# Weight scales of a low-rank feed-forward made for two chunks at a time, in products of 256 columns instead of 128

## The chip, the cores and the metric

The kernel runs on one core of a Trainium2 chip. The metric is the device time of one execution, in microseconds (us). The core has TensorE (PE, matmuls; PEld is its weight load), VectorE (DVE), ScalarE (ACT), GpSimd (POOL) and SyncE (SP), which issues nearly all DMAs here. Each engine works through its own list of instructions in order, and waits at semaphores for the others. Matmul results lie in PSUM, eight banks of 128 x 512 float32; only two of them, numbers 6 and 7, are at stake here.

## What is computed

2048 tokens of width 512 go through a small state-space stack of four layers, a feed-forward, an attention of 32 heads, and the same feed-forward again, each on a normalized input and added to x. The change touches the first feed-forward alone. Its weights are products of a raw matrix and a low-rank matrix of scales:

```python
B, S, H, I, R = (4, 32, 512, 1792, 4)

def _anemll_linear(x, w, su, sv):
    w_eff = w * (su @ sv)
    return jnp.einsum('bsh,oh->bso', x, w_eff)
a = _anemll_linear(x, gate_w, gate_su, gate_sv)
b = _anemll_linear(x, up_w, up_su, up_sv)
d = jax.nn.silu(a) * b
return _anemll_linear(d, down_w, down_su, down_sv)
...
x = x + _L0_attn_a_ref(_layernorm(x, axis=-1), ...)
x = x + _L0_ffn_ref(_layernorm(x, axis=-1), ...)
x = x + _L0_attn_b_ref(_layernorm(x, axis=-1), ...)
x = x + _L0_ffn_ref(_layernorm(x, axis=-1), ...)
```

## The kernel before

**Tiling.** The 1792 inner columns of the feed-forward are 14 chunks of 128 (IC = 14). The tokens are four blocks of 512 (T = 0 to 3). The first feed-forward runs over the steps n = 14 T + i. The first block, T = 0, makes the effective weights of its chunks as it goes, and saves them in HBM; the later blocks load them.

**One chunk, in steps.** The planner's names are used below, with the chunk's number behind them (gate4, smul9).
- `fetch`: SP loads the raw weights of the chunk (gate, up and down, 3 x 512 columns, 768 KB) into one of the two slots of the buffer `stage`. It waits until the steps `gulo` and `dnlo` of the chunk two before are done with that slot.
- `scale`, three parts: PE multiplies the low-rank factors. For gate and up (parts 0 and 1) that is four products of 128 columns each, one for each piece of 128 input rows (line 1812; the chunk's 128 columns of `long_st` are the moving operand, `short_st` the stationary one). For down (part 2) it is one product of 512 columns (L1815). A part fills one of the two PSUM banks 6 and 7, the pool "bank". The same two banks serve the stack's own products of the sequences s = 1 to 3 and, for T = 1 to 3, the transposed tiles (`fxT`).
- `smul`, three parts: DVE multiplies 512 columns of `stage` in place by the bank (L1530), which frees the bank.
- `guhi` and `gulo`: the rounded part of gate and up (ACT, L1302) and the remainder (DVE, L1534) go to one of three slots `wgu`; `dnhi` and `dnlo` (L1309, L1539) do the same for down in `wdn`. `saveg` and `saved` are SP's DMAs of them to HBM (L1127, L1130).
- `gate` and `up`, each in two halves of six products of 512 columns (L837), then `gsilu` (ACT), `d` (DVE), `dhi`, `dlo`, and `down` in two halves.

**The stack beside it.** The state-space stack runs for four sequences of tokens. Sequence 0 is on the way to the first `gate` (the lead); the others are filled in between the feed-forward's steps. Of one norm and layer: `var` (L1918), `eps` (DVE, L1751), `rstd` (POOL, L1262), `wide` (ACT, L1446), `rtr` (PE, L1934), `yn`, `silu`, `ui` (POOL, L1270) and `ur`, two scans `zr` and `zi`, `pi` (POOL, L1273), `pr`, `prs` (L1784), then `conv` (PE; L1944 for s = 2 and 3), `h`, and, for the layer's feed-forward, `w1` (L1959) and `w2` (L1971). `proj` (L1911) begins a sequence. `bout` (POOL, L1292) adds a bias to a tile of x; there are 12 of them behind the lead.

**What sets the order.** The class `Steps` is a list scheduler that runs when the program is built. Each step has an engine, an assumed duration, predecessors with gaps, and an urgency; PSUM banks are a pool. It picks the step that can begin first, then by urgency, and so writes each engine's list. A change to the durations or predecessors of `scale` and `smul` can thus move any step of the phase.

## Time and profile before

| what | value |
| --- | --- |
| time, median of 3 runs | 2368.31 us (2368.25 to 2370.93) |
| the profiled execution's own time | 2372.38 us |
| its span in the trace | 2371.1 us |
| PE busy | 2328.1 us (98%) |
| DVE, ACT, POOL busy | 1589.5, 1218.3, 838.5 us |
| chain that ended last | PE 93%, DVE 2%, the rest 1% or less each |
| bytes moved by DMA | 444.84 MB |

The profile page gives busy time by engine and the chain of work that ended last; busy time by stretch gives the same for pieces of the span, with TensorE's granted clock (1.00 is 2.4 GHz, 0.50 is 1.2). In a timeline, a row is a run of like instructions: its start, its length, the engine, the line, what it writes and reads, the count, and in brackets how long the engine stood idle before it and whose result ended that. Lengths of neighbouring matmuls overlap, so the cost of a matmul in a dense run is read from one start to the next.

### The profile page before, as it was taken

The page shows a single profiled execution, that of the slowest core. Times are in us where ns is not written, and L with a number is a line of the kernel's source. Part 1 is how long each engine was busy: PE and PEld are TensorE (multiplying, and loading weights), DVE is VectorE, ACT ScalarE, POOL GpSimd, SP SyncE. Part 2 cuts the span into 40 slices and gives each one's busy share as a digit, 9 for nine tenths or more (in the row PEclk, how much of TensorE's full clock was granted, in tenths as well). Part 3 has the DMA queues.
Part 4 walks back from the last instruction along what each step waited for, and adds up shares of the span by engine and source line. Part 5 has one row for each costly group of instructions (what it writes and reads, how often), then busy time and mean ns, then how long its engine had stood idle before and what let it go on. Part 6 is the DMA issues. An engine that isn't in the chain of part 4 may idle for free.

```text
span 2371.1 us, 40814 instructions
## 1 busy us (share of the span) xinstructions
PE 2328.1 (98%) x12672; PEld 2015.7 (85%) x12672; DVE 1589.5 (67%) x3900; ACT 1218.3 (51%) x3827; POOL 838.5 (35%) x1332
## 2 busy tenths in 40 slices
PE   6899999999999999999999999999999999999999
PEld 4577777888899999999999999999999988888887
DVE  7666664534277777777777777777777776565553
ACT  7543332233266666666666666766766661232212
POOL 5550443212034445444454554444544440010000
PEclk8899999999999999999999999999999999999999
DMA  4335567987831534536346346364362225565554
GB/s 144 105 144 199 203 237 281 346 342 280 314 125 63 236 145 164 231 139 233 147 150 235 124 157 244 131 231 165 137 249 92 95 70 204 189 219 195 189 192 160
DMA packets 92627, 444.84 MB, mean 188 GB/s; under 512 B 10168, under 2 KB 17336, under 8 KB 72704
## 3 DMA queue, kind: packets, MB, share of 16 engines
q1 hardware_dynamic: 91056, 440.78, 50.5%
q8 instruction: 106, 1.74, 0.3%
q10 hardware_dynamic: 1360, 1.46, 0.2%
q14 instruction: 105, 0.86, 0.1%
HBM read 342.59 MB, written 99.61 MB: 186 GB/s over the span
## 4 chain that ended last, share of the span: by engine, by line
PE 93%; DVE 2%; DMA 1%; ACT 1%; POOL 1%; issue 1%; SPq 0%; DVEq 0%; POOLq 0%; ACTq 0%
PE psum L837 80%; PE psum L2832 4%; PE psum L2786 2%; PE psum L2821 1%; PE psum L2822 1%; PE psum L2777 1%; POOL x L1292 0%; POOL srstd L1262 0%; DMA wD<-weff_dn 0%; DMA short_raw<-in_lr_short 0%; DMA weff_s<-short_st 0%; PE psum L1812 0%; PE psum L1981 0%; PE psum L1959 0%; PE psum L1971 0%
## 5 line engine op out<-in xcount | busy, mean ns | idle before, releaser
L837 PE MATMUL psum<-qw,xs 128*128 128x384 f32 x2688 | 548.6, 346 | 0.2 <-DVE su L2630 0.2
L837 PEld LDWEIGHTS psum<-qw,xs 128*128 128x128 f32 x2688 | 457.8, 188 | 1.0 <-issue 0.4
L2603 POOL TENSOR_SCALAR prob<-prob,rsum 128x128 f32<-128x128 f32 (+1 forms) x512 | 228.9, 460 | 527.3 <-DVE rsum L2711 527.2
L2545 ACT ACTIVATE prob<-biased,nmax 128x256 f32<-128x256 f32 (+1 forms) x512 | 227.2, 446 | 151.0 <-DVE nmax L2701 147.7
L2719 DVE TENSOR_TENSOR oT_l<-psum,oT_h 128x512 fp32r<-128x512 f32 x128 | 88.5, 692 | 193.9 <-ACT oT_h L2557 193.9
L837 PE MATMUL psum<-wo_h,oT_h 128*128 128x512 f32 x512 | 208.5, 407 | 0.0
L837 PE MATMUL psum<-wo_l,oT_h 128*128 128x512 f32 x512 | 203.5, 397 | 0.0
L837 PE MATMUL psum<-wo_h,oT_l 128*128 128x512 f32 x512 | 202.0, 394 | 0.0
L2486 ACT ACTIVATE squares<-cc 128x128 f32<-128x128 f32 x512 | 154.3, 305 | 41.0 <-DVE cc L2633 31.4
L2552 ACT ACTIVATE pT_h<-psum 128x384 fp32r<-128x384 f32 x256 | 125.2, 489 | 76.1 <-PE psum L2832 73.7
L2569 POOL TENSOR_TENSOR rr<-ss,mneg_half 128x6 f32<-128x6 f32 (+1 forms) x128 | 150.1, 1173 | 10.7
L837 PE MATMUL psum<-xT0h,wgu 128*128 128x512 f32 x448 | 151.2, 399 | 1.4 <-DVE svar L1751 1.4
L837 PE MATMUL psum<-xT1h,wgu 128*128 128x512 f32 x448 | 147.9, 395 | 0.0
L2714 DVE TENSOR_TENSOR pT_l<-psum,pT_h 128x384 fp32r<-128x384 f32 x256 | 141.7, 553 | 8.1 <-ACT pT_h L2552 1.8
L837 PE MATMUL psum<-xw_h,wS 128*128 128x512 f32 x448 | 147.0, 389 | 0.0
L2699 DVE SCALAR_TENSOR_TENSOR low_bias<-alibi,q_root,psum 128x128 f32<-128x128 f32 x256 | 88.4, 345 | 49.0 <-PE psum L2822 48.2
L2832 PE MATMUL psum<-ident,prob 128*128 128x128 f32 x768 | 116.8, 274 | 0.0
L837 PEld LDWEIGHTS psum<-wo_h,oT_l 128*128 128x128 f32 x512 | 96.1, 188 | 23.8
L837 PE MATMUL psum<-xw_h,wA 128*128 128x512 f32 x336 | 112.6, 389 | 0.0
L837 PEld LDWEIGHTS psum<-wo_h,oT_h 128*128 128x128 f32 x512 | 96.4, 188 | 17.1 <-DVE oT_l L2719 0.5
L837 PE MATMUL psum<-kT,qT_h 128*128 128x256 f32 x512 | 109.3, 295 | 0.0
L837 PEld LDWEIGHTS psum<-wo_l,oT_h 128*128 128x128 f32 x512 | 96.5, 189 | 14.2
(360 smaller groups left out, 5863.9 us busy)
## 6 DMA issues: line engine op xcount, KB each, us to landing
xs<-weff_x SPq DMA_DIRECT2D x62, 1792.0 KB, 7.9
wgu<-weff_gu SPq DMA_DIRECT2D x42, 1024.0 KB, 7.4
qw<-weff_q SPq DMA_DIRECT2D x56, 768.0 KB, 7.8
weff_q<-q_parts SPq DMA_DIRECT2D x84, 384.0 KB, 2.4
wD<-weff_dn SPq DMA_DIRECT2D x56, 512.0 KB, 4.8
wS<-weff_s SPq DMA_DIRECT2D x28, 1024.0 KB, 7.2
wdn<-weff_dn SPq DMA_DIRECT2D x42, 512.0 KB, 4.6
weff_gu<-wgu SPq DMA_DIRECT2D x14, 1024.0 KB, 4.0
```

Of the source, the lines that this page charges most:

```text
L837: ins = pe.matmul(out_ap, stat[a], mov[b], start=start and n == 0, stop=stop and n == last)
L2486: ins = act.activation(squares[:, first_place + hd, :], cc[:, tile, half, (hd + 1) * HD:(hd + 2) * HD], ACT.Square, accum_out=ss[:, n:n + 1])
L2545: act.activation(prob[:, b, lo:hi], biased[:, b % 2, lo:hi], ACT.Exp, bias=nmax[:, b, t:t + 1], scale=-1.0, accum_out=esum[:, b, t:t + 1]) ...
L2552: act.activation(pT[0][:, b % 2, :], psum[:, b, 0:SC], ACT.Copy).then_inc(pT_hi, 1)
L2569: pool.tensor_tensor(rr[:, part], ss[:, part], mneg_half[:, 0:part.stop - part.start], ALU.pow).then_inc(r_done if b else r_part, 1)
L2603: pool.tensor_scalar(prob[:, b, lo:hi], prob[:, b, lo:hi], rsum[:, b, t:t + 1], 1.0, ALU.mult, ALU.mult).then_inc(prob_done, 1)
L2699: dve.scalar_tensor_tensor(out=low_bias[:, b % 2, :], in0=alibi[:, b, 0:P], scalar=q_root[:, b:b + 1], in1=psum[:, b, SC:SC + P], op0=ALU. ...
L2714: dve.tensor_tensor(pT[1][:, b % 2, :], psum[:, b, 0:SC], pT[0][:, b % 2, :].bitcast(F32), ALU.subtract).then_inc(pT_lo, 1)
L2719: dve.tensor_tensor(oT[1][:, hs, :], psum[:, 2 * b, :].rearrange("p (h c) -> p h c", h=2), oT[0][:, hs, :].bitcast(F32), ALU.subtract).the ...
L2777: ins = pe.transpose(psum[:, across_bank(what, a, b), t * P:(t + 1) * P], cc[:, t, 0, 0:HD], ident[:])
L2786: ins = pe.transpose(psum[:, across_bank(what, a, b), hd * P:(hd + 1) * P], q_heads(b)[:, hd // 2, hd % 2, :], ident[:])
L2832: ins = pe.transpose(psum[:, b, k * P:(k + 1) * P], prob[:, b, k * P:(k + 1) * P], ident[:])
```

## The change

The scales and the multiplications of chunks n and n + 1 (n even) are one job of six parts. Parts 0 to 3 are gate and up: a part covers two of the four pieces of 128 input rows for both chunks, as two products of 256 columns (the 256 columns of `long_st` of both chunks), and fills one bank. Its `smul` multiplies 2 x 256 columns in both slots of `stage` at once, and waits for both raw chunks. Parts 4 and 5 are the down scales of chunk n and n + 1, one product of 512 columns each. `guhi` of either chunk waits for part 3, `dnhi` for its own part of 4 and 5. The planner is given 0.24 us for each part of `scale`.

```diff
                 if made:
-                    before = [("gulo", n - 2, 0), ("dnlo", n - 2, 0)] if n >= 2 else [(("begin", 0, 0), 16.0)]
-                    o.add(("fetch", n, 0), "sp", 0.7, before, 3)
-                    for part in range(3):
-                        chain = [("scale", n, part - 1)] if part else [("scale", n - 1, 2)] if n else []
-                        o.add(("scale", n, part), "pe", 0.45 if part < 2 else 0.23, [("lr", 2, 0), ("lr", 2, 1), ("lr", 3, 0), ("lr", 3, 1),
-                              ("lr", 3, 2), (("fetch", n, 0), 6.5)] + chain, 3, ("bank", 1))
-                        o.add(("smul", n, part), "dve", 0.69, [("scale", n, part), (("fetch", n, 0), 6.5)], 3, None,
-                              ("scale", n, part))
+                    m = n - n % 2
+                    if n == m:
+                        for k in (n, n + 1):
+                            before = [("gulo", k - 2, 0), ("dnlo", k - 2, 0)] if n else [(("begin", 0, 0), 16.0)]
+                            o.add(("fetch", k, 0), "sp", 0.7, before, 3)
+                        for part in range(6):
+                            chain = [("scale", n, part - 1)] if part else [("scale", n - 2, 5)] if n else []
+                            there = [(("fetch", k, 0), 6.5) for k in ((n, n + 1) if part < 4 else (n + part - 4,))]
+                            o.add(("scale", n, part), "pe", 0.24, [("lr", 2, 0), ("lr", 2, 1), ("lr", 3, 0), ("lr", 3, 1),
+                                  ("lr", 3, 2)] + there + chain, 3, ("bank", 1))
+                            o.add(("smul", n, part), "dve", 0.69, [("scale", n, part)] + there, 3, None, ("scale", n, part))
...
-                    o.add(("guhi", n, 0), "act", 1.06, [("smul", n, 1)] + (
+                    o.add(("guhi", n, 0), "act", 1.06, [("smul", m, 3)] + (
...
-                    o.add(("dnhi", n, 0), "act", 0.63, [("smul", n, 2), ("guhi", n, 0)] + (
+                    o.add(("dnhi", n, 0), "act", 0.63, [("smul", m, 4 + n % 2), ("guhi", n, 0)] + (
...
-                act.wait_ge(aux_free, aux_freed["smul", a, 1])
+                act.wait_ge(aux_free, aux_freed["smul", a - a % 2, 3])
...
             elif what == "smul":
-                part = stage[:, a % 2, b * DM:(b + 1) * DM]
                 dve.wait_ge(scale_mm, 3 * a + b + 1)
-                dve.wait_ge(raw_in[a % 2], 16 * (a // 2 + 1))
-                dve.tensor_tensor(part, part, psum[:, spare(("scale", a, b)), :], ALU.mult).then_inc(aux_free, 1)
+                for c in (0, 1) if b < 4 else (b - 4,):
+                    dve.wait_ge(raw_in[c], 16 * (a // 2 + 1))
+                scales = psum[:, spare(("scale", a, b)), :]
+                if b < 4:
+                    part = stage[:, :, b * 2 * P:(b + 1) * 2 * P].rearrange("p c (k i) -> p c k i", k=2)
+                    scales = scales.rearrange("p (k c i) -> p c k i", k=2, c=2)
+                else:
+                    part = stage[:, b - 4, 2 * DM:]
+                dve.tensor_tensor(part, part, scales, ALU.mult).then_inc(aux_free, 1)
...
-                cols_ = slice(a * P, (a + 1) * P)
-                if b < 2:
-                    for k in range(KC):
-                        ins = pe.matmul(psum[:, bank, k * P:(k + 1) * P], short_st[:, b, k * P:(k + 1) * P],
-                                        long_st[:, cols_], start=True, stop=True)
+                if b < 4:
+                    kind, first_k = divmod(2 * b, KC)
+                    for k in range(2):
+                        rows = slice((first_k + k) * P, (first_k + k + 1) * P)
+                        ins = pe.matmul(psum[:, bank, k * 2 * P:(k + 1) * 2 * P], short_st[:, kind, rows],
+                                        long_st[:, a * P:(a + 2) * P], start=True, stop=True)
                 else:
-                    ins = pe.matmul(psum[:, bank, :], long_st[:, cols_], short_st[:, b, :], start=True, stop=True)
+                    cols_ = slice((a + b - 4) * P, (a + b - 3) * P)
+                    ins = pe.matmul(psum[:, bank, :], long_st[:, cols_], short_st[:, 2, :], start=True, stop=True)
```

PE's list ahead of gate8, first before the change: two parts of chunk 9's scales, the eight runs of down6 (`wdn_106`), a `w1` of the stack, and gate8 (`wgu_105`).

```order
L1812 MATMUL psum<-long_st,short_st 128x128 x4
L1815 MATMUL psum<-short_st,long_st 128x512
L837 MATMUL psum<-wdn_106,dT0h 128x512 x2
L837 MATMUL psum<-wdn_106,dT0l 128x512
L837 MATMUL psum<-wdn_106,dT0h 128x512 x2
L837 MATMUL psum<-wdn_106,dT0l 128x512
L837 MATMUL psum<-wdn_106,dT0h 128x512 x2
L837 MATMUL psum<-wdn_106,dT0l 128x512
L837 MATMUL psum<-wdn_106,dT0h 128x512 x2
L837 MATMUL psum<-wdn_106,dT0l 128x512
L1959 MATMUL psum<-buf_e_98,w_sb 128x256 x4
L837 MATMUL psum<-xT0h,wgu_105 128x512
```

The same place after the change: scale8.1, the second half of down6, then scale8.2 to scale8.5 in a row, `conv` and `var` of the stack, and gate8.

```order
L1839 MATMUL psum<-ident,xn 128x128 x4
L1822 MATMUL psum<-long_st,short_st 128x256 x2
L840 MATMUL psum<-wdn_106,dT0h 128x512 x2
L840 MATMUL psum<-wdn_106,dT0l 128x512
L840 MATMUL psum<-wdn_106,dT0h 128x512 x2
L840 MATMUL psum<-wdn_106,dT0l 128x512
L1822 MATMUL psum<-long_st,short_st 128x256 x4
L1826 MATMUL psum<-short_st,long_st 128x512 x2
L1955 MATMUL psum<-buf_c_90,center_s 128x256
L1929 MATMUL psum<-blk_mean,buf_b_87 128x2 x2
L840 MATMUL psum<-xT0h,wgu_105 128x512
```

The scales of chunk 8, which stood several chunks ahead of gate8, now stand directly in front of it, together with those of chunk 9. DVE's list at the same place, before: the transposed tiles of block 1 (L1523), chunk 9's multiplications and remainders (`wgu_103`), then those of chunk 10.

```order
L1530 TENSOR_TENSOR stage<-stage,psum 128x512
L1523 TENSOR_TENSOR xT1l<-psum,xT1h 128x4x128 x2
L1547 TENSOR_TENSOR d<-gate,psum 128x512
L1530 TENSOR_TENSOR stage<-stage,psum 128x512 x2
L1551 TENSOR_TENSOR dT1l<-d,dT1h 128x512
L1534 TENSOR_TENSOR wgu_103<-stage,wgu_103 128x1024
```

And after: all of the pair's multiplications but the first are behind the tiles, and the remainder of chunk 8 (`wgu_105`) behind all six.

```order
L1556 TENSOR_TENSOR d<-gate,psum 128x512
L1526 TENSOR_TENSOR xT1l<-psum,xT1h 128x4x128
L1560 TENSOR_TENSOR dT1l<-d,dT1h 128x512
L1539 TENSOR_TENSOR stage<-stage,psum 128x2x256
L1526 TENSOR_TENSOR xT1l<-psum,xT1h 128x4x128
L1539 TENSOR_TENSOR stage<-stage,psum 128x2x256 x2
L1539 TENSOR_TENSOR stage<-stage,psum 128x512 x2
L1543 TENSOR_TENSOR wgu_105<-stage,wgu_105 128x1024
```

So gulo8 comes last in the pair's work on DVE. The third place is POOL's list behind the lead's last norm. Before, `rstd` (srstd) and `bout` (x) alternate:

```order
L1262 TENSOR_TENSOR srstd<-svar,mneg_half 128x4
L1292 TENSOR_TENSOR x<-x,bout_sb 128x512 x3
L1262 TENSOR_TENSOR srstd<-svar,mneg_half 128x4
L1292 TENSOR_TENSOR x<-x,bout_sb 128x512
L1262 TENSOR_TENSOR srstd<-svar,mneg_half 128x4
L1292 TENSOR_TENSOR x<-x,bout_sb 128x512 x7
L1270 TENSOR_TENSOR buf_b_86<-buf_e_98,rot 128x256
L1262 TENSOR_TENSOR srstd<-svar,mneg_half 128x4
```

After, sequence 3 of the stack has been begun earlier, and ten `bout` stand in a row ahead of the next `rstd`, which is rstd1.4:

```order
L1265 TENSOR_TENSOR srstd<-svar,mneg_half 128x4 x2
L1295 TENSOR_TENSOR x<-x,bout_sb 128x512 x10
L1265 TENSOR_TENSOR srstd<-svar,mneg_half 128x4
L1273 TENSOR_TENSOR buf_b_86<-buf_e_98,rot 128x256
L1295 TENSOR_TENSOR x<-x,bout_sb 128x512 x2
```

What moved here is `bout` relative to `rstd`. In PE's list the rtr1.4 that needs this `rstd` now stands between gate1 and up1; before, it stood three halves later, between the halves of down0.

## Rows read from the trace of the kernel before

**Rows 1.** The page: busy time by engine, share of the span, instructions

```profile
PE 2328.1 (98%) x12672; PEld 2015.7 (85%) x12672; DVE 1589.5 (67%) x3900; ACT 1218.3 (51%) x3827; POOL 838.5 (35%) x1332
```

**Rows 2.** Busy by stretch: length; PE, PEld, DVE, ACT, POOL (instructions); clock, DMA share, GB/s

```profile
117.28:149.68 32.40, 30.38 (x150) 23.48 (x151) 21.78 (x37) 12.87 (x24) 26.06 (x22) 1.00 0.28 106
149.68:210.54 60.86, 60.86 (x317) 46.84 (x316) 41.84 (x73) 22.64 (x37) 9.08 (x10) 1.00 0.50 177
```

**Rows 3.** Gate and up scale products: duration ns min/median/max, first and last start

```profile
L1812 PE MATMUL psum<-long_st,short_st x112: 220/274/668, 45.7 to 244.9; 128*128 128x128 f32 x112
```

**Rows 4.** Timeline of PE (start, length): eight scale products of 128, what follows

```profile
213.40 1.00 PE L1812 MATMUL psum<-long_st,short_st 128*128 128x128 f32 x8
214.24 0.45 PE L837 MATMUL psum<-xT0h,wgu 128*128 128x512 f32 x1
```

**Rows 5.** Timeline of PE: products of 512 and of 256 columns in the attention

```profile
1053.53 0.40 PE L837 MATMUL psum<-pT_h,v_l 128*128 128x512 f32 x1
1053.76 0.27 PE L837 MATMUL psum<-pT_h,v_h 128*128 128x256 f32 x1
1053.88 0.28 PE L837 MATMUL psum<-pT_l,v_h 128*128 128x256 f32 x1
```

**Rows 6.** Timeline of PE: steps of the stack between gates (var, conv, w1, w2, rtr)

```profile
146.82 0.50 PE L1918 MATMUL psum<-blk_mean,buf_b 128*128 128x2 f32 x4
147.18 0.68 PE L1944 MATMUL psum<-buf_c,center_s 128*128 128x256 f32 x2
...
151.26 1.14 PE L1959 MATMUL psum<-buf_e,w_sb 64*128 64x256 f32 x8
...
155.31 1.08 PE L1971 MATMUL psum<-hidden,w_c 128*64 128x256 f32 x8
...
162.17 0.38 PE L1934 MATMUL psum<-ident,buf_b 128*128 128x128 f32 x2
```

**Rows 7.** Timeline of PE at the slower clock, and the start of the first gate

```profile
65.28 1.12 PE L1812 MATMUL psum<-long_st,short_st 128*128 128x128 f32 x4
66.19 1.16 PE L1948 MATMUL psum<-buf_c,center_s 128*128 128x256 f32 x2
...
117.28 0.47 PE L837 MATMUL psum<-xT0h,wgu 128*128 128x512 f32 x1 [1.42 <-DVE svar L1751]
```

**Rows 8.** Instructions on the buffer stage, 117 to 250 us: ns min/median/max

```profile
L1530 DVE TENSOR_TENSOR stage<-stage,psum x27: 656/681/689, 149.7 to 246.9; 128x512 f32<-128x512 f32 x27
L1302 ACT ACTIVATE wgu<-stage x11: 1042/1060/1062, 125.1 to 246.7; 128x1024 fp32r<-128x1024 f32 x11
L1534 DVE TENSOR_TENSOR wgu<-stage,wgu x11: 1212/1222/1871, 126.1 to 247.8; 128x1024 fp32r<-128x1024 f32 x11
```

**Rows 9.** Timeline of POOL behind the lead: bout in a row, then rstd1.4

```profile
114.97 3.75 POOL L1292 TENSOR_TENSOR x<-x,bout_sb 128x512 f32<-128x512 f32 x3 [0.19 <-DVE xn L1515]
...
121.90 10.46 POOL L1292 TENSOR_TENSOR x<-x,bout_sb 128x512 f32<-128x512 f32 x7
...
133.40 1.02 POOL L1262 TENSOR_TENSOR srstd<-svar,mneg_half 128x4 f32<-128x4 f32 x1
```

**Rows 10.** Busy by stretch, around the last drop of the clock; columns as in rows 2

```profile
94.60:101.50 6.90, 4.94 (x35) 2.93 (x34) 3.95 (x9) 3.25 (x7) 4.26 (x4) 1.00 0.00 0
101.50:108.30 6.80, 5.79 (x18) 2.82 (x19) 2.55 (x5) 2.28 (x6) 1.04 (x2) 0.50 0.01 2
110.70:117.30 6.60, 4.87 (x41) 3.75 (x41) 4.63 (x11) 4.46 (x9) 4.91 (x6) 1.00 0.00 0
```

**Rows 11.** DMA issues from 117 to 262 us: size, median us to landing; then one fetch

```profile
weff_gu<-wgu SPq DMA_DIRECT2D x11, 1024.0 KB, 3.9
stage<-in_ffn_w SPq DMA_DIRECT2D x9, 768.0 KB, 5.8
...
DMA to landing us min/median/max: 8.1/8.1/8.1
```

**Rows 12.** Timeline of PE: the wait of conv3.3

```profile
344.12 0.67 PE L1944 MATMUL psum<-buf_c,center_s 128*128 128x256 f32 x2 [1.89 <-DVE buf_c L1784]
```

More of the change, by code:

```diff
@@ L531, in ffn_steps @@
                         o.add(("shi", n, 0), "act", 1.1, [("wcomb", n, 0)] + (
-                            [(("saves", n - 1, 0), 5.0)] if i else [("scale", IC - 1, 2)]), 6)
+                            [(("saves", n - 1, 0), 5.0)] if i else [("scale", IC - 2, 5)]), 6)
                         o.add(("slo", n, 0), "dve", 1.25, [("shi", n, 0)], 6)
@@ L1304, in act_ffn @@
                 r = a % WSLOTS
-                act.wait_ge(aux_free, aux_freed["smul", a, 2])
+                act.wait_ge(aux_free, aux_freed["smul", a - a % 2, 4 + a % 2])
                 if a >= WSLOTS:
```

## The prediction, made before the changed kernel had run

> **What bounds the kernel now.** I read the page first, then busy time by stretch, then PE's waits, then timelines of single places. PE is busy for 2328.1 of 2371.1 us, so the time moves by what PE executes and by what it waits, and by little else [rows 1]. The change acts between 45 and 245 us, where the scale products run [rows 3], and there the stages differ. Up to the first gate at 117.28 us [rows 7] the lead sequence of the stack is a chain of latencies over all engines. From there to 149.68 PE is busy for 30.38 of 32.40 us; from 149.68 on it is full, 60.86 of 60.86 us to the start of gate8 [rows 2]. In the full stretch a product removed is time gained, if nothing waits in its place. DVE has room on average there (41.84 of 60.86), but an average says nothing on whether a chunk's weights are ready when PE comes to its gate. That is the question of this change.
>
> **Scale products.** In a dense run eight products of 128 columns take 0.84 us from start to start (213.40 to 214.24), 0.105 each [rows 4]. No product of 256 columns exists in the scales; the nearest are those of the attention, split in rounded parts and remainders as here, 0.12 from start to start, and 0.23 for 512 columns [rows 5]. So a part of four by 128 costs 0.42 us and a part of two by 256 about 0.235, for the same number of outputs. In the full stretch, before: chunks 5 to 13, 18 parts by 0.42 = 7.6 us. After: the scales of chunk 4 have moved into it, so it is five pairs, 20 parts by 0.235 = 4.7, and one down product more, 0.23. Term A: -7.6 + 4.7 + 0.2 = **-2.7 us**. Ends: 0.21, which is 0.42 halved, and 0.27 for a part with a tenth lost at each change of operand, -3.2 to -2.0.
>
> The Trainium skill speaks against term A: its page "TensorE: Matmul & The Clock Gate", section "Back-to-back issue gap", gives N/2.4 + 2.5 ns for a product of N columns at the full clock, as an isolated gap. That is 56 ns for 128 columns and 109 for 256, so four of the one would cost what two of the other do, and term A would be about +0.6 us, an estimate from that page. The measured 105 ns for 128 columns is nearly twice the page's figure and the 120 ns for 256 is close to it; the row decides, and term A stands.
>
> **Stack steps that the planner moved.** With less to place ahead of the first gate (chunk 4's parts are gone, chunk 3's are cheaper), it starts sequence 3 earlier: var3.0, rtr3.0 and conv3.0 leave the full stretch. Such a var takes 0.36 us to the next start, a conv of sequences 2 and 3 and an rtr 0.3 and 0.2, their lengths less the overlap [rows 6]. Term B: **-0.9 us**.
>
> **Ahead of the first gate.** PE's scale work lies mostly in idle time there, except where the clock is at 1.2 GHz: four products from 65.28 to 66.19 take 0.91 us [rows 7], and a second part stands behind them, both in front of conv0.2 of the lead. At that clock two parts by 256 take 0.9 to 1.0 in place of 1.8, so the lead gains 0.9 us; later scale3.1 and scale3.2 are gone in front of w20.2, 0.65 us by rows 4 and 5, of which I count 0.6. Against it the earlier sequence 3 puts one step of its own on DVE, ACT and POOL each in front of the lead's last norm, estimated at 0.4 us. The rest cancels. Term C: **-1.1 us**; since a drop of the clock there may fall elsewhere, ends -2.5 and +1.5.
>
> **POOL's queue behind the lead.** Ten bout now stand in front of rstd1.4. Three took 3.75 us and seven 10.46 [rows 9], so ten take 14 from 115; rstd1.4 (1.02) is done at 130, wide1.4 at 130.4. PE reaches rtr1.4 after six halves of 1.4 us (six products by 0.23 [rows 5]), a w1, a w2 and three small steps, 3.2 us together [rows 6], counted from 117.0: at 128.6. It waits 1.8 us there, and by the same count 0.5 at conv2.1 and 0.5 at rtr3.1. In return the 2.0 us that PE stood idle in this stretch go [rows 2]. Term D: 2.8 - 2.0 = **+0.8 us** (0 to +2).
>
> **The lost double buffer.** Of two slots both now belong to one pair. The multiplications wait for both raw chunks; guhi of the even chunk waits for four parts instead of two; and gulo of the even chunk is queued on DVE behind all six. What waits for that is PE at gate4, gate6 and gate8. A multiplication takes 0.68 us, guhi 1.06, gulo 1.22 [rows 8]; in a row DVE's overlap a little, 0.62 from start to start.
> - Gate 8. Counted from the end of down6, scale8.2 and scale8.3 each need a bank that DVE frees (smul8.1, the tile fxlo1.3), then scale8.4 and scale8.5 the banks of smul8.2 and smul8.3. DVE works from 0.4 us on without a gap: smul8.2, 8.3, 8.4, 8.5 by 0.62, that is to 3.0, then gulo8, to 4.3. PE has 0.95 of scales, conv2.2 and var3.2 (0.7) to do: 1.6. It waits 2.7 us.
> - Gate 4. scale4.5 stands behind the first half of down2, smul4.5 and a scan (1.1 us) ahead of gulo4, about 3.4 us with the lags; PE has the second half of down2 and a w1 (2.5 us) as cover. It waits 0.9 us. Gate 6 has smul6.4 and 6.5 and no scan, 2.6 us, against a half and two rtr, 1.8: 0.8 us.
> - Gates 10 and 12. Here three and five halves lie between the last part and the gate, so gulo is hidden. But fetch10 and fetch11 leave SP together behind two saves. A fetch lands after 5.8 us in the median and the one behind a save after 8.1 [rows 11]; two of each would put the second near 9 to 10 us after gulo9, and scale10.2 needs the bank of smul10.0, which waits for it. It waits 1 us (0 to 2).
>
> Odd gates have a whole chunk of PE work, over 8 us, as cover. Term E: 2.7 + 0.9 + 0.8 + 1.0 = **+5.4 us**. If the real lists run with more lead on DVE than I count, it is 3; if the fetches are late at each pair, 9.
>
> The multiplication with 2 x 256 columns in pieces of 128 has the same count of elements, so I take it at L1530's 0.68 us. The wait on two raw chunks costs nothing at the other pairs, where by the same count the second fetch is issued some 8 us before its use or more.
>
> **Further on.** conv3.3 waited 1.89 us [rows 12]. It now stands about seven halves of PE work behind rtr3.6 instead of nine, but without a weight sum in front of its silu and ui; I make its wait 1.3. Term F: **-0.6 us** (-1.9 to +1.5). Behind it the lists are alike and PE is full, so a shift goes through to the end.
>
> **Sum.** -2.7 - 0.9 - 1.1 + 0.8 + 5.4 - 0.6 = +0.9 us against the span of 2371.1, or the execution's 2372.38: 2373.3. The median of the runs lies 4.1 us below that execution (2368.31), so I forecast **2369 us**, in a word, no change. 0.2% of this kernel, 4.7 us, is about what a measurement can tell from no change.
>
> **Rivals.**
> - *The covers hold.* PE comes to the even gates later than I count, because the stack steps between cost more than their rows say, and E shrinks to 1 or below. Then -2.7 - 0.9 - 1.1 + 0.8 + 0.5 - 0.6 = -4.0: 2364, and 2363 if D goes too. For it: each change of operand between the steps costs PE a little that I leave out. Against it: DVE's work at gate 8 hangs on down6's end itself, by the banks, and shifts along.
> - *The pair starves (slower).* The second fetch of a pair is issued only when dnlo of the odd chunk is through. If it lands later than PE's second part of scales, DVE, then PE by the banks, wait at each of the five pairs. The landing time of 5.8 us leaves about 8 at most of them; from some 9 us on each pair costs what is over. At 10 to 11 us for all, five by 1.5 to 2 more: E = 14, sum +9: 2377. For it: 8.1 behind one save. Against it: only pair 10 has two saves directly ahead.
> - *The clock drops.* TensorE's clock was at 1.2 GHz from 101.5 to 108.3 us, behind a stretch in which PE was busy for 4.94 of 6.90 us; in another with 4.87 of 6.60 it stayed at 2.4 GHz [rows 10]. Around gate 8 PE would be idle for some 3 of 6 us. A drop of 6.8 us in a full stretch takes 3.4 more: +4.3, 2372.4, and with a second drop slower than 0.2%.
> - *256 columns cost twice 128*, so that the change does not do what it says. Then A is +0.8 by 20 parts of 0.42: sum +4.4, 2372.5. By the rule quoted above the sum would be alike. Rows 4 and 5 speak against it.
>
> **Chances.** Forecast 0.62; covers hold 0.16; starving 0.10; clock 0.09; 256 columns 0.03. The forecast's own range is 2365 to 2373. Of "covers hold" about half passes 4.7 us, with the forecast's lower tail 0.12 for faster; slower gets the starving pairs, half of the clock's case and a little of the upper tail, 0.17; the same 0.71. The range 2363.5 to 2374 leaves out part of the outer cases.
>
> **What would show it.** Products of 256 columns at 0.11 to 0.12 us from start to start, not 0.21. Gate 0 near 116. A wait of PE on POOL's or ACT's side at rtr1.4 of 1 to 2 us. PE idle before gate4, gate6 and gate8, ended by DVE's `wgu` (L1543), the longest at gate8, and waits of scale8.4 and 8.5 on `stage`. The stretch 149.68 to 210.54, with 60.86 busy of 60.86 before, would show 3 to 6 us idle. The prediction is wrong if these idles are absent, if the pairs wait for DMA, or if the last gate of block 0 starts over 4 us earlier or later than before with all waits as said.

## The result, and the profile after

| what | before | changed |
| --- | --- | --- |
| time, median of the runs taken together | 2369.57 us (7 runs, 2367.69 to 2376.11) | 2379.55 us (7 runs, 2375.98 to 2381.37) |
| ratio to before | | 1.0036, 95% interval 1.0026 to 1.0047 |
| the profiled execution, and its span | 2372.38, 2371.1 us | 2380.47, 2379.1 us |

The change makes the kernel slower, by about 8.5 us as a ratio and 8.0 us between the two profiled spans. The forecast was 2369.0 us, with a range from 2363.5 to 2374.0. The result lies above it, and the case that was given the best chance, no change (0.71), did not come.

The page of the changed kernel, busy time by engine, to be read beside [rows 1]: PE is busy for 1.1 us less, though the span is 8.0 us longer. So what was added is time in which PE waits; the busy time also holds stretches at the slow clock, which come up below.

```profile
PE 2327.0 (98%) x12616; PEld 2014.4 (85%) x12616; DVE 1590.9 (67%) x3900; ACT 1218.0 (51%) x3827; POOL 834.9 (35%) x1332
```

Busy time of PE by stretch, first of the changed kernel, then of the kernel before (length; PE busy and instructions, granted clock, DMA share, GB/s). The cuts are at 63.9 us, at the first gate, at gate8, and at a point behind which the two lists of PE are alike.

```profile
63.90:122.26 58.36, 43.84 (x268) 0.85 0.26 92
122.26:223.14 100.88, 94.86 (x476) 1.00 0.32 118
223.14:358.00 134.86, 133.45 (x633) 0.98 0.67 242
358.00:2379.10 2021.10, 2013.12 (x11023) 1.00 0.51 191
```

```profile
63.90:117.28 53.38, 43.85 (x276) 0.87 0.28 93
117.28:210.54 93.26, 91.24 (x465) 1.00 0.42 153
210.54:350.00 139.46, 137.57 (x684) 1.00 0.62 224
350.00:2371.10 2021.10, 2014.19 (x11026) 1.00 0.51 190
```

The reading: the first gate starts 5.0 us later (122.26 against 117.28), all of it lost between 63.9 us and there, with the same busy time (43.84 against 43.85 us). From the first gate to the last cut the changed kernel needs 3.0 us more (235.74 against 232.72): its waits grew from 3.91 us (2.02 + 1.89) to 7.43 (6.02 + 1.41), and its busy time fell from 228.81 to 228.31. Behind the last cut both need 2021.10 us. So 5.0 + 3.0 = 8.0.

PE's waits in the changed kernel, in its timeline; the first one is on the lead, the second is the first gate:

```profile
74.60 0.80 PE L1822 MATMUL psum<-long_st,short_st 128*128 128x256 f32 x2 [4.62 <-DVE stage L1539]
...
122.26 0.47 PE L840 MATMUL psum<-xT0h,wgu 128*128 128x512 f32 x1 [1.62 <-DVE xT0l L1526]
...
140.51 0.67 PE L1955 MATMUL psum<-buf_c,center_s 128*128 128x256 f32 x2 [1.83 <-DVE buf_c L1793]
...
166.61 1.14 PE L1970 MATMUL psum<-buf_e,w_sb 64*128 64x256 f32 x8 [0.46 <-DVE stage L1539]
168.34 0.50 PE L840 MATMUL psum<-xT0h,wgu 128*128 128x512 f32 x1 [0.60 <-DVE wgu L1543]
...
184.58 1.14 PE L1970 MATMUL psum<-buf_e,w_sb 64*128 64x256 f32 x8 [1.34 <-DVE stage L1539]
...
196.30 0.50 PE L840 MATMUL psum<-xT0h,wgu 128*128 128x512 f32 x1 [0.48 <-DVE wgu L1543]
...
220.13 1.10 PE L1826 MATMUL psum<-short_st,long_st 128*128 128x512 f32 x2 [0.50 <-DVE stage L1539]
221.41 0.70 PE L1955 MATMUL psum<-buf_c,center_s 128*128 128x256 f32 x2 [0.18 <-DVE stage L1539]
...
223.14 0.79 PE L840 MATMUL psum<-xT0h,wgu 128*128 128x512 f32 x1 [0.53 <-DVE wgu L1543]
...
258.39 1.10 PE L1822 MATMUL psum<-long_st,short_st 128*128 128x256 f32 x4 [1.31 <-DVE stage L1539]
```

The largest is scale2.2, which stands in front of var0.5 of the lead. It waits for a bank that smul2.0 frees. The timeline of DVE in the changed kernel shows what smul2.0 waits for:

```profile
68.56 0.41 DVE L1752 TENSOR_TENSOR h<-h,psum 128x256 f32<-128x256 f32 x1
73.86 1.28 DVE L1539 TENSOR_TENSOR stage<-stage,psum 128x512 f32<-128x512 f32 x2 [4.89 <-DMA stage<-in_ffn_w]
```

It waits for raw weights. In the kernel before, no multiplication waited for a DMA; the view of its multiplications (L1530) names PE alone as what DVE sat idle for (us, times):

```profile
  PE psum L1812: 7.5, 6
  PE psum L1815: 2.0, 4
```

The timeline of SP (the issues), and the busy times of the 15 us in which the raw weights of chunks 2 and 3 are under way (here the columns are those of [rows 2]):

```profile
58.80 1.46 SPq L1130 DMA_DIRECT2D weff_gu<-wgu  x2
60.61 0.90 SPq L1085 DMA_DIRECT2D stage<-in_ffn_w  x1
61.55 1.47 SPq L1133 DMA_DIRECT2D weff_dn<-wdn  x1
63.12 1.81 SPq L1085 DMA_DIRECT2D stage<-in_ffn_w  x1
```

```profile
58.80:73.80 15.00, 8.10 (x54) 5.05 (x54) 8.51 (x16) 12.53 (x32) 6.02 (x8) 0.95 0.87 315
```

The last fetch, issued at 63.12, stands behind two saves of 1 MB, a fetch of 768 KB and a save of 512 KB. With itself that is some 4 MB, moved at 315 GB/s with the DMA engines 0.87 busy. Of this fetch alone, the summary of `stage` has a landing time of 10.6 us, so it is there at 73.7, where smul2.0 starts:

```profile
DMA to landing us min/median/max: 10.6/10.6/10.6
```

The pairs of chunks 6 and 12 have the same pattern: their second fetches, issued at 172.6 and 247.0 us, land 10.5 us later each, and behind them stand the waits of 1.34 and 1.31 us at 184.58 and 258.39. A late landing alone makes no wait: those of the pairs 8 and 10 took 10.4 and 9.4 us, and no multiplication waited for them. The Trainium skill, page "DMA: Bandwidth & Descriptors", section "Queues, rings and completion order", says that each DMA engine consumes the descriptors of a queue in their order. By that, a load behind four transfers is taken up after them, and the late landings agree with it; no row shows the order itself.

Last, the clock. At the waits of gate8 a stretch of the changed kernel began that ran at 1.2 GHz (granted clock 0.50), in which a product of 512 columns took 0.43 us from start to start in place of 0.23. In the kernel before there was none behind the first gate. The stretch, and the one ahead of it:

```profile
215.70:222.50 6.80, 6.02 (x30) 1.00 0.01 2
222.50:229.30 6.80, 6.27 (x17) 0.50 0.83 302
```

### The profile page after: what moved, and what is told of

It reads as the page before. It is cut to its first block, busy times and chain, and to the rows that moved or that the text cites. A ratio compares the mean times of both kernels' runs of the same rounds, so it can differ in the third digit from the quotient of the medians.

```text
span 2379.1 us, 40702 instructions
## 1 busy us (share of the span) xinstructions
PE 2327.0 (98%) x12616; PEld 2014.4 (85%) x12616; DVE 1590.9 (67%) x3900; ACT 1218.0 (51%) x3827; POOL 834.9 (35%) x1332
## 4 chain that ended last, share of the span: by engine, by line
PE 90%; DMA 4%; DVE 3%; ACT 1%; issue 1%; SPq 1%; POOL 0%; DVEq 0%; ACTq 0%
PE psum L840 78%; PE psum L2843 4%; PE psum L2797 2%; DMA stage<-in_ffn_w 1%; PE psum L2832 1%; DMA weff_s<-short_st 1%; PE psum L2833 1%; PE psum L2788 1%; DMA short_raw<-in_lr_short 0%; DMA stage<-in_wqkv 0%; PE psum L1970 0%; PE psum L1929 0%; PE psum L1982 0%; PE psum L1992 0%; DVE stage L1539 0%
## 5 line engine op out<-in xcount | busy, mean ns | idle before, releaser
L2730 DVE TENSOR_TENSOR oT_l<-psum,oT_h 128x512 fp32r<-128x512 f32 x128 | 88.5, 691 | 193.7 <-ACT oT_h L2568 193.6
L2580 POOL TENSOR_TENSOR rr<-ss,mneg_half 128x6 f32<-128x6 f32 (+1 forms) x128 | 150.3, 1174 | 10.6
```

Source lines behind the costliest of these rows:

```text
L2580: pool.tensor_tensor(rr[:, part], ss[:, part], mneg_half[:, 0:part.stop - part.start], ALU.pow).then_inc(r_done if b else r_part, 1)
L2730: dve.tensor_tensor(oT[1][:, hs, :], psum[:, 2 * b, :].rearrange("p (h c) -> p h c", h=2), oT[0][:, hs, :].bitcast(F32), ALU.subtract).the ...
```

## Experiments

Each row of the table has its ratio to runs of the kernel before that were taken on the same chip; medians in us. The median of the kernel before was 2370.71 us beside e1 to e4, 2370.79 beside e5 to e8 and 2372.06 beside e9 to e11, so across these groups the ratios say more than the medians. The first gate and the granted clock from 60 us to it are of the one profiled execution. "Against" is the kernel from which it differs by one thing.

| kernel | median | ratio, 95% interval | first gate | clock | against |
| --- | --- | --- | --- | --- | --- |
| before | 2369.57 | | 117.28 | 0.88 | |
| changed | 2379.55 | 1.0036 (1.0026 to 1.0047) | 122.26 | 0.86 | |
| e1_fetch_first | 2369.40 | 0.9992 (0.9984 to 1.0001) | 114.56 | 0.91 | changed |
| e2_split | 2381.88 | 1.0046 (1.0033 to 1.0059) | 123.66 | 0.87 | changed |
| e3_pairs_from_4 | 2371.37 | 0.9999 (0.9990 to 1.0008) | 116.75 | 0.91 | changed |
| e4_fill | 2378.37 | 1.0028 (1.0017 to 1.0039) | 122.87 | 0.84 | changed |
| e5_tiles_later | 2363.45 | 0.9970 (0.9959 to 0.9981) | 115.71 | 0.91 | e1 |
| e6_pair_2_only | 2371.20 | 0.9999 (0.9989 to 1.0010) | 115.19 | 0.91 | changed |
| e7_first_split | 2374.11 | 1.0013 (1.0005 to 1.0022) | 114.38 | 0.94 | e1 |
| e8_before_fetch_first | 2372.22 | 1.0004 (0.9994 to 1.0014) | 115.19 | 0.94 | before |
| e9_before_tiles_later | 2367.46 | 0.9983 (0.9974 to 0.9992) | 116.28 | 0.94 | before |
| e10_bout_later | 2369.85 | 0.9996 (0.9987 to 1.0005) | 117.31 | 0.91 | e5 |
| e11_first_fill | 2368.02 | 0.9980 (0.9971 to 0.9990) | 115.53 | 0.91 | e1 |

**The fetches first.** After the planner has run, both fetches of a pair are put ahead of the saves on SP's list:

```diff
         order1 = first.ordered(patient=PATIENT)
+        def ahead(engine, key, *steps):
+            for k in steps:
+                order1[engine].remove(k)
+            at = order1[engine].index(key)
+            order1[engine][at:at] = steps
+        for m, key in ((2, ("saveg", 0, 0)), (6, ("saveg", 4, 0)), (10, ("saveg", 8, 0)), (12, ("saveg", 10, 0))):
+            ahead("sp", key, ("fetch", m, 0), ("fetch", m + 1, 0))
```

> The changed kernel; only SyncE's list differs: both raw fetches of the pairs 2, 6, 10 and 12 stand ahead of the saves that were in front of them. Nothing moves on PE, DVE, ACT or POOL. Theory (the pair starves for bytes): the second raw chunk lands 10.5 us after its issue because two to four saves of 0.5 and 1 MB are being moved ahead of it, and scale2.2 (4.62 us), w11.3 behind scale6.1 (1.34) and scale12.2 (1.31) wait for nothing else. Then fetch 3 lands some 6 us after its issue, the three waits go or shrink below 0.5 us each, and the time falls by 4 to 7 us, to 2373 to 2376 (ratio to the kernel before 1.001 to 1.003). Rival (the waits only show DVE's own lateness, the lost double buffer): another wait takes their place, and the time stays within 2 us of 2379.5.

It gave 2369.40 us, 10 us below the changed kernel and more than the 4 to 7 expected. Its timelines of SP, DVE and PE, at the place where the changed kernel waited:

```profile
60.65 1.82 SPq L1093 DMA_DIRECT2D stage<-in_ffn_w  x2
62.51 0.90 SPq L1138 DMA_DIRECT2D weff_gu<-wgu  x2
```

```profile
69.31 1.28 DVE L1547 TENSOR_TENSOR stage<-stage,psum 128x512 f32<-128x512 f32 x2 [0.29 <-DMA stage<-in_ffn_w]
```

```profile
70.05 0.51 PE L1830 MATMUL psum<-long_st,short_st 128*128 128x256 f32 x2
...
114.56 0.47 PE L848 MATMUL psum<-xT0h,wgu 128*128 128x512 f32 x1 [1.76 <-DVE xT0l L1534]
```

The second fetch lands after 7.6 us (some 6 were expected), smul2.0 starts at 69.31 in place of 73.86, PE does not wait, and neither do the places behind the pairs 6 and 12. The first gate starts 7.7 us earlier than in the changed kernel. That is more than the wait of 4.62: the changed kernel's lead also ran at 1.2 GHz from 72.3 us on, which is inside that wait (it ends at 74.60), and e1 ran at 2.4 GHz there. This row is of the changed kernel:

```profile
72.30:82.60 10.30, 8.00 (x34) 6.54 (x36) 5.96 (x13) 1.96 (x3) 5.12 (x7) 0.50 0.02 10
```

So the theory stands and its price was too low. The table shows the same split: the three leads that starve (changed, e2, e4) have a clock of 0.84 to 0.87 from 60 us to the first gate, the seven in which the fetch comes in time, e3 included, have 0.91 to 0.94. By length of the stretches that is 17 to 20 us at 1.2 GHz against 7 to 10. The kernel before, which does not starve, lies between with 13.7 us (0.88), and with 6.8 in e8 and e9 (0.94), so the clock of the lead also varies by itself. What each microsecond beyond the wait belongs to is only argued, since PE is not full on the lead and the slow stretches fall in other places.

**Where the starving costs most.** e6 moves only the fetches of chunks 2 and 3:

```diff
+        ahead("sp", ("saveg", 0, 0), ("fetch", 2, 0), ("fetch", 3, 0))
```

> The changed kernel with only the fetches of chunks 2 and 3 moved ahead of the saves of chunks 0 and 1 on SyncE's list; the pairs 6, 10 and 12 as in the changed kernel. Theory: most of e1_fetch_first's 10 us is the wait of 4.6 us on the lead and what hangs on it (first gate at 114.6 in place of 122.3 us); the waits of 1.3 us at w11.3 and scale12.2 stay. Time 2371 to 2374, that is 2 to 4 us above e1_fetch_first and 6 to 9 below the changed kernel. Rival (the pairs in the full stretch weigh as much): 2375 or more.

2371.20 us: 8.35 of e1's 10.15 us come from this one pair, since it sits on the lead. The wait behind pair 6 is still there with 0.73 us, the one at scale12.2 is gone in this execution; the rest, 1.8 us between the medians, is not separated by the intervals. The two waits in the full stretch are marginal altogether. With the same order of fetches and saves at pair 6, its second fetch lands after 10.5 us in e4 and e6 (wait 0.73 us both times) and after 9.1 and 8.5 in e2 and e3 (no wait of 0.3 us or more); at pair 12 it lands after 8.9 to 9.3 in these four, and none has a wait at scale12.2. Only the changed kernel's profiled execution shows both at full size.

e3 comes at the same place from the other side: chunks 0 to 3 are made one at a time, as before, and pairs begin with chunk 4.

```diff
-                    if n == m:
+                    if n < 4:
+                        before = [("gulo", n - 2, 0), ("dnlo", n - 2, 0)] if n >= 2 else [(("begin", 0, 0), 16.0)]
+                        o.add(("fetch", n, 0), "sp", 0.7, before, 3)
+                        for part in range(3):
...
+                    elif n == m:
```

> The changed kernel with chunks 0 to 3 made one at a time as before, pairs only from chunk 4 on. Up to w20.2 of the lead the lists of all engines are then those of before, and from the first gate on those of the changed kernel. Theory (the step of the prediction that failed is the lead, term C): no wait of 4.6 us at scale2.2, the first gate starts at 117 to 119 us instead of 122.26, and the time falls by 3.5 to 5.5 us, to 2374 to 2376. Rival (the loss lies in the full stretch, gates 4 to 12, and the lead's is given back later): 2378 to 2380.

2371.37 us with the first gate at 116.75: the lead is repaired, and more is gained than expected. The rival falls. e1, with pairs on the lead that do not starve, reaches its first gate 2.2 us earlier than e3. That is one profiled execution of each, and leads without pairs reach it at 115.19 to 117.28 us (before, e3, e8, e9), so the pairs' own worth on the lead is smaller than such a single difference can show.

**The control.** e8 is the kernel before with fetches 2, 3, 12 and 13 moved ahead of saves in the same way.

```diff
+        for m, key in ((2, ("saveg", 0, 0)), (3, ("saveg", 1, 0)),
+                        (12, ("saveg", 10, 0)), (13, ("saveg", 11, 0))):
+            ahead("sp", key, ("fetch", m, 0))
```

> Control: the kernel before, with the fetches 2, 3, 12 and 13 each moved ahead of the saves in front of it on SyncE's list. In the kernel before no multiplication waits for raw data in the trace. Theory (the order of the fetches matters only to a kernel that works in pairs): no change, ratio 0.999 to 1.001. Rival (part of e1_fetch_first's gain is the order of the DMAs and has nothing to do with the pairs): 2 us or more faster.

Ratio 1.0004: no change. Where the chunks are made one at a time, the order of the fetches is worth nothing that these runs can tell.

**What the wider products are worth.** Both e2 (from the changed kernel) and e7 (from e1) make each product of 256 columns as two of 128:

```diff
                     for k in range(2):
                         rows = slice((first_k + k) * P, (first_k + k + 1) * P)
-                        ins = pe.matmul(psum[:, bank, k * 2 * P:(k + 1) * 2 * P], short_st[:, kind, rows],
-                                        long_st[:, a * P:(a + 2) * P], start=True, stop=True)
+                        for c in range(2):
+                            ins = pe.matmul(psum[:, bank, (2 * k + c) * P:(2 * k + c + 1) * P], short_st[:, kind, rows],
+                                            long_st[:, (a + c) * P:(a + c + 1) * P], start=True, stop=True)
```

> The changed kernel; each product of 256 columns is made as two of 128 columns with the same weights, in the same place, everything else alike. Term A as forecast (0.105 us per 128 columns, 0.12 per 256): a part costs 0.42 in place of 0.24, 20 parts behind the first gate cost 3.7 us more, of which what lies beside waits of PE (up to 1.2 us at gate 8 and some at gates 4 and 6) is hidden: +2 to +4 us against the changed kernel, 2381.5 to 2383.5. Rival (256 columns cost what two of 128 do, as the rule of the Trainium skill in the prediction has it): no change, 2379.5 within 1 us.

> e1_fetch_first with each product of 256 columns made as two of 128. Theory: with the starving waits gone nothing hides the longer parts but the 1 us at gates 4, 6 and 8, so term A shows almost whole: +3 to +5 us against e1_fetch_first, 2372.5 to 2374.5, where e2_split had shown +2.3 over the changed kernel. Rival (256 columns cost twice 128, the skill's rule): 2369.4 within 1 us.

e2 is 2.3 us above the changed kernel, with intervals that overlap; e7 is 4.7 above e1, with intervals apart. The difference between the two is as expected (without starving nothing hides the longer parts), but the overlap leaves e2's own size open. e7's profiled execution is the fastest of its twelve (2369.77 us) and has no slow stretch between the first gate and the attention, where e1's has 6.8 us; PE is busy there for 551.50 us in e7 and 550.54 in e1, so at a like clock e7 has some 4.4 us more to do, an estimate that counts e1's slow stretches at half their length. The timelines of PE show the size. Changed kernel, a part alone between two gates' products, and two parts in a row with what follows:

```profile
156.90 0.51 PE L1822 MATMUL psum<-long_st,short_st 128*128 128x256 f32 x2
157.24 0.39 PE L840 MATMUL psum<-xT0h,wgu 128*128 128x512 f32 x1
...
236.58 0.64 PE L1822 MATMUL psum<-long_st,short_st 128*128 128x256 f32 x4
237.05 0.40 PE L840 MATMUL psum<-xT0h,wgu 128*128 128x512 f32 x1
```

e7, a part alone:

```profile
203.10 0.64 PE L1831 MATMUL psum<-long_st,short_st 128*128 128x128 f32 x4
203.58 0.45 PE L848 MATMUL psum<-xT0h,wgu 128*128 128x512 f32 x1
```

Two parts in a row take 0.47 us from start to start, 0.235 each and 0.12 for a product, as in term A. A part that stands alone takes 0.34 as two of 256 and 0.48 as four of 128. So the gain is 0.14 to 0.185 us a part. The Trainium skill, page "TensorE: Matmul & The Clock Gate", section "Back-to-back issue gap", gives N/2.4 + 2.5 ns for an isolated product at the full clock, by which two of 128 columns cost what one of 256 does, and says itself that this counts too little at small N in a stream of weight loads and products. In these products (operands in tiles of type fp32r, each with a weight load of its own) two of 128 cost 0.21 us and one of 256 costs 0.12, so the isolated gap is the wrong price here.

**The clock at gate8.** e4 (from the changed kernel) and e11 (from e1) put four products that nobody reads into the two longer of PE's waits at gate8. They write into the bank that gate8 begins anew.

```diff
             if what == "scale":
+                if (a, b) == (8, 4):
+                    pe.wait_ge(gate_done, 8)
+                    for _ in range(2):
+                        pe.matmul(psum[:, GATE, :], long_st[:, 0:P], short_st[:, 2, :], start=True, stop=True)
                 wait_bank((what, a, b))
...
                 if b == 0 and what == "gate":
+                    if a == 8:
+                        pe.wait_ge(gate_done, 8)
+                        for _ in range(2):
+                            pe.matmul(psum[:, GATE, :], long_st[:, 0:P], short_st[:, 2, :], start=True, stop=True)
```

> The changed kernel with four products of 512 columns that nobody reads (into the bank that gate8 then begins anew): two ahead of scale8.4 and two ahead of gate8, in places where PE waits 0.50 and 0.53 us. They take 0.46 us each two. Theory (idle time at gate 8 lets the clock fall to 1.2 GHz from 222.5 to 229.3 us, which costs 3.4 us): the clock stays at 2.4 GHz there and the time falls by 2.5 to 3.4 us, to 2376 to 2377. Rival (the fall has another cause, or the profiled execution is not typical): the clock falls as before, and the time is 2379.5 to 2380.5.

> e1_fetch_first with the four unread products of e4_fill at gate8, two ahead of scale8.4 and two ahead of gate8; PE's waits there are filled and nothing else moves. Theory (the clock falls behind gate8 for 3.4 to 6.8 us in most executions, which costs 1.7 to 3.4 us each): no such fall, and the median 1 to 3 us below e1_fetch_first's 2369.4, 2366.5 to 2368.5. Rival (falls happen by chance somewhere anyway, the fill only adds its products): 2369 to 2370.

Busy time of PE by stretch around gate8, of e4, of e11, then of e1, e3 and e6, which have the waits unfilled, and of e7, unfilled as well:

```profile
218.00:238.00 20.00, 19.58 (x94) 1.00 0.60 209
```

```profile
211.00:225.00 14.00, 13.68 (x64) 1.00 0.47 146
```

```profile
215.70:219.00 3.30, 3.07 (x8) 0.60 0.23 26
```

```profile
216.90:220.20 3.30, 3.30 (x10) 0.52 0.95 392
```

```profile
216.90:223.60 6.70, 6.19 (x16) 0.50 0.83 303
```

```profile
212.00:226.00 14.00, 12.86 (x63) 1.00 0.45 133
```

The profiled executions of the changed kernel, e1, e2, e3 and e6 have a slow stretch at gate8, of 3.4 or 6.8 us; those of e4 and e11 have none. e7's has none either, with waits of 0.34, 0.18 and 0.53 us, where e2 with 0.33, 0.18 and 0.53 has one. So the idle time goes with the fall and does not force it. There is a second such place: right behind the wait of conv2.1, a stretch of 3.4 us at 1.2 GHz begins in e1 (at 134.5 us), e4 (142.5) and e6 (135.0), after waits of 2.11, 2.11 and 2.10 us, and none in e3 and e7 after 2.11 and 2.08. Between the first gate and the attention e11's profiled execution is 2.4 us shorter than e1's (553.58 against 556.02), but only half of e1's 6.8 slow us are at gate8. In the medians, e4 is 1.2 us below the changed kernel (1.9 by ratio) and e11 1.4 below e1 (2.8 by ratio), and the intervals overlap in both cases; the 2.5 to 3.4 us expected of e4 did not come. Both point the same way, with a size of 1 to 3 us. The profiles show two executions without the fall where the waits are filled, and five of six with it where they are not; the share of all executions in which it happens is not shown.

**Room at gate8.** In e5, which is e1 with one edit more, the planner ranks the tiles of block 1 behind the scale parts. The line stands for each T, so the edit ranks those of blocks 2 and 3 lower as well, which both expectations below leave out:

```diff
-                urgent = 0 if T == 0 else 1
+                urgent = 0 if T == 0 else 4
```

> e1_fetch_first, and the planner gives the four tiles of block 1 (fxT1.0 to fxT1.3, frow and fxlo with them) a lower urgency, so that the scale parts of chunk 8 come ahead of them: the last of the parts then stands ahead of down6 instead of right ahead of gate8. Theory (term E at gate 8 is DVE's chain of multiplications and gulo8 behind the banks, and the idle there lets the clock fall): the waits of 0.50, 0.18 and 0.53 us around gate8 go, no stretch at 1.2 GHz follows gate8, and the time falls by 1 to 4 us against e1_fetch_first, to 2366 to 2368.5 (ratio to the kernel before 0.998 to 0.999). Rival (the tiles, queued on DVE and on the two banks behind, make PE wait further on; or the fall of the clock only moves): within 1 us of 2369.4.

> Control: the kernel before, and the planner gives the tiles of block 1 the lower urgency of e5_tiles_later. Before, PE waits for nothing from gate3 to gate14, so a place for the tiles further back can give nothing there. Theory (e5_tiles_later's gain over e1_fetch_first comes from the waits at gate8 that the pairs made): ratio to before 0.999 to 1.001. Rival (the tiles' place is a gain of its own): 3 us or more faster than before, as e5_tiles_later over e1_fetch_first was (5.9 us).

e5 gave 2363.45 us, better than expected, and is the fastest kernel of the study. Its parts of chunk 8 end ahead of down6, and gate8 starts with no wait at full clock; PE's busy time by stretch and the timeline:

```profile
205.00:225.00 20.00, 20.00 (x105) 1.00 0.55 189
```

```profile
208.33 0.62 PE L1834 MATMUL psum<-short_st,long_st 128*128 128x512 f32 x2
208.78 0.61 PE L848 MATMUL psum<-wdn,dT0h 128*128 128x512 f32 x2
...
212.29 0.48 PE L848 MATMUL psum<-xT0h,wgu 128*128 128x512 f32 x1
```

But the control fell: e9, the kernel before with the same edit, is faster than before by 4 us (0.9983), where I had expected nothing. In its trace the wait of conv3.3 [rows 12] is gone. From the first gate to the first product of the attention it takes 551.82 us with 1.99 idle, where the kernel before takes 554.90 with 3.90: 1.9 us less waiting and 1.2 us less busy time. That wait can cost more than its 1.89 us: in e8, which has it too, this profile shows a slow clock right behind it, and products of 512 columns 0.43 us apart.

```profile
342.01 0.67 PE L1953 MATMUL psum<-buf_c,center_s 128*128 128x256 f32 x2 [1.95 <-DVE buf_c L1793]
...
343.02 1.05 PE L846 MATMUL psum<-xT1h,wgu 128*128 128x512 f32 x2
```

So the place of the tiles is a gain of its own. In e1 the wait of conv3.3 was gone already, so e5's gain over e1 (5.9 us by medians, 5.2 by ratio) is not that one. Between the same two points e1 takes 556.02 us with 5.48 idle and 6.8 at 1.2 GHz, e5 550.12 with 2.90 idle and 3.4 at 1.2 GHz: 5.9 us less, of which 2.6 are waits (1.21 of them at gate8), 1.7 the clock at half the difference, and 1.6 a smaller busy time of the kind that e9 shows too. Why the tiles' place makes PE's busy time smaller, and which block's tiles do it, is not shown. With both kernels given the later tiles, e5 against e9, the pairs are worth about 3 us (0.9970 against 0.9983), and the intervals overlap.

**POOL's queue.** e10 is e5 with the bout of sequences 2 and 3 held until ui2.1:

```diff
-                o.add(("bout", s, t), "pool", 1.27, [("fold", 5, 0), ("row", s, t), ("w1", 0, t) if lead else ("frow", 0, TPB - 1)], 6)
+                o.add(("bout", s, t), "pool", 1.27, [("fold", 5, 0), ("row", s, t), ("w1", 0, t) if lead else ("frow", 0, TPB - 1) if s == 1 else ("ui", 2, 1)], 6)
```

> e5_tiles_later, with the eight bout of sequences 2 and 3 allowed on POOL only after ui2.1, so that four bout instead of ten stand in front of rstd1.4. Theory (term D: the waits of 1.35 to 2.1 us at conv2.1 are POOL's queue of bout): that wait goes, and with the order further on like that of e5_tiles_later the time falls by 1 to 2 us, to 2361.5 to 2362.5. Rival (the planner's new order behind it, with the scale parts of chunks 4 and 6 a little later against their gates, makes new waits at gate4 and gate6 worth as much): 2363 to 2366.

2369.85 us, 6.4 above e5: the rival, and more. PE's waits in the first stretch did not go, they spread over four places (1.28, 1.51, 0.76 and 0.55 us, where e5 has one of 1.35), and gate6 got waits of its own, with a slow clock of 3.4 us from 193.7 us on, inside the last of them. In the timeline of PE:

```profile
133.70 0.41 PE L1953 MATMUL psum<-ident,buf_b 128*128 128x128 f32 x2 [1.28 <-ACT buf_b L1457]
138.36 0.67 PE L1963 MATMUL psum<-buf_c,center_s 128*128 128x256 f32 x2 [1.51 <-DVE buf_c L1801]
...
194.18 0.79 PE L848 MATMUL psum<-xT0h,wgu 128*128 128x512 f32 x1 [1.36 <-DVE wgu L1551]
```

The run does not isolate term D, since the planner moved everything behind it.

## Why the prediction was wrong

**The step that failed** is the last sentence on term E, with its echo in term C: "The wait on two raw chunks costs nothing at the other pairs, where by the same count the second fetch is issued some 8 us before its use or more". At pair 2 the second fetch was issued 5.9 us before smul2.0 wanted it and landed after 10.6; at pair 6 it landed after 10.5 as well. But for pair 10, the landing time was taken as a property of a fetch (5.8 us in the median [rows 11]) and not as the time for the bytes that share the queue with it. The prediction had named "if the pairs wait for DMA" as a sign of being wrong, and that sign came. In the old order one fetch shares the queue with the saves of one chunk. In pairs, two chunks' saves and two fetches leave together, about 4 MB, and the last of them waits for all. The "rest" of the lead that was said to cancel held this wait, in front of var0.5, where nothing covers it. The rival "the pair starves" had the mechanism and its landing time of 10 to 11 us right. Its argument against, "only pair 10 has two saves directly ahead", was a mistake: pair 10 landed after 9.4 us, as forecast, and is one of those that did not starve. And its place was wrong. It counted five pairs in the full stretch, of which two showed 1.3 us each, and left out pair 2 on the lead, which cost most; that its 2377 us came nearest is partly luck.

By its steps, in the profiled executions:
- **A and B**, -3.6 us together. Busy time from the first gate to the last cut fell by 0.5 us, and the slow stretch of 6.8 us in it costs up to 3.4 (3.1 if its 0.53 us of waiting cost nothing more): so -3.6 to -3.9. Right in size, though found as a remainder; e7 confirms A's sign and size apart.
- **C**, -1.1 us. Measured +5.0: 6.1 us off, the largest error. With the fetches first the first gate is at 114.38 to 115.71 us in e1, e5, e6, e7 and e11, 115.1 in the mean, and at 117.31 in e10, whose plan differs; without pairs on the lead it is at 117.28, 116.75, 115.19 and 116.28 in the kernel before, e3, e8 and e9, 116.4 in the mean. The difference of 1.3 us (0.9 with e10) fits the term for a lead that does not starve, but the two groups touch.
- **D**, +0.8 us. conv2.1 waits 1.83 us and the old 2.02 are gone: -0.2. The wait came at conv2.1, not at rtr1.4.
- **E**, +5.4 us. The waits at 166.61, 168.34, 184.58, 196.30, 220.13, 221.41, 223.14 and 258.39 are 0.46 + 0.60 + 1.34 + 0.48 + 0.50 + 0.18 + 0.53 + 1.31 = 5.40 us. The agreement is luck. Gate8 was to cost 2.7 and cost 1.21, since DVE's multiplications kept step with the scale parts better than counted. Gate4 has 1.06 (0.9) and gate6 0.48 (0.8). 1.34 and 1.31 us are starving at pairs 6 and 12; the term had 1.0 for gates 10 and 12 on that ground, where gate10 had no wait, and nothing for pair 6.
- **F**, -0.6 us. The wait of conv3.3 is gone, -1.9.
- **The clock**, a rival with a chance of 0.09: it came as described, 6.8 us at gate8 for 3.4 us. It should have had a large chance, given waits there of the size that I forecast myself.

Together -3.9 + 5.0 - 0.2 + 5.4 - 1.9 + 3.4 = 7.8 us, against 8.0 between the spans. That the sum closes tests nothing about the clock, whose 3.4 us stand in it twice with opposite signs. Without the starving on the lead and at the pairs, e1 has 2369.4 us beside the forecast's 2369.0. By ratio it is 1.9 us below the kernel before (3.8 below to 0.2 above), where the sum had 0.9 above, so the rest of the sum was right within some 3 us, with errors that offset each other: in e1's profile E is 2.75 us (5.4 forecast), F -1.9 (-0.6), D +0.1 (+0.8), and the clock costs up to 3.4 (nothing). The claim made without a row decided the result.

The other rivals: that the covers hold, no, the waits were there; that 256 columns cost twice 128, no. That rival's term A leaves out the one down product more: it is +1.0 us and not +0.8, which changes nothing else.

## What to carry to other kernels

When work is batched, its transfers are batched too: the last load of a batch landed late because of the bytes that stood in the queue ahead of it, so work out its landing from those bytes and a measured rate, and put the loads that someone waits for ahead of the stores that nobody does. Leave a margin: with the fetches first, a fetch with only 768 KB ahead still took 7.6 us, with 3 MB of saves issued right behind it. A cost found at nothing needs the same row as any other: for each wait that a change adds, look up when its signal comes at every place where it stands, the latency-bound lead first. A short idle time of PE in a dense stretch can cost its length and then a slow clock on top. The order alone can be worth as much as the products: ranking the tiles lower gave 4.0 us in the old kernel (e9) and 5.2 in e1 (e5, by ratio), the wider products 4.7 (e7). And a control can fall: it was e9 that showed that the place of the tiles gives some 4 us without any pairs.

## What the runs showed of the hardware

- A fetch of 768 KB landed after 4.2 us with nothing ahead of it (e1, chunk 2), 5.8 in the median of the kernel before, and 10.4 to 10.6 with 3.3 MB issued in the 5 us ahead of it, at 315 GB/s (changed kernel, chunks 3, 7, 9 and 13). For a transfer in a queue the size in front counts for more than its own. What comes behind it counts too: in e1 a fetch with nothing ahead landed after 5.3 us when the saves followed it at once (chunk 13), and one with 768 KB ahead and saves right behind after 7.1 and 7.6 (chunks 11 and 3).
- Idle times of some 0.5 us and less at gate8, three within 4 us, were followed in five of six profiled executions by 3.4 or 6.8 us at 1.2 GHz, which began 2.3 to 3.6 us behind the end of the first of them. PE was busy for 6.02 of the 6.80 us ahead of the fall in the changed kernel. Single waits of 2.1 us at conv2.1 were followed by such a fall in three of five. The waits of 1.34 and 1.31 us at 184.58 and 258.39 were followed by none. What decides between them is open.
- A product of 256 columns in fp32r starts 0.12 us after the one before it and two of 128 take 0.21 in a row of eight, but a part that is enclosed by products with other operands takes 0.34 and 0.48 us where the row would have it at 0.235 and 0.42. The loss is at the change, 0.1 us for the part of two and 0.06 for the part of four (once, at 181.46 in the changed kernel, a part of two took 0.24 and lost nothing).
